# Filing stage of a graph layer: statistics of x two tiles ahead, and the preparation of edge keys in four pieces

## The reference

```
xn = layernorm(x)                                  # (x - mean) / sqrt(var + 1e-5), per row
x  = x + gnn(xn, edges) + mix(xn)                  # two graph convolutions; linear attention, 8 heads
x  = x + ffn(layernorm(x))                         # 8 experts, top 2
# a graph convolution, over the edges in both directions:
agg = segment_sum(x[src], dst) / max(deg, 1)
y   = x @ W0 + b0 + agg @ W1 + b1
```

## Time and profile before

| | us |
|---|---|
| median of 3 runs | 2323.24 |
| lowest, highest | 2322.51, 2326.59 |
| the profiled execution | 2325.6 |
| its span | 2324.1 |
| filing stage in it, first `onehots` to last `ranks` | 38.28 to 392.74 |
| first matmul of the next stage (L2222) | 430.86 |

### The profile page before, as it was taken

How to read it: one execution, slowest core, us unless ns; L and a number is a source line. 1 busy time by engine, 2 the same in 40 slices (tenths; PEclk the granted TensorE clock), 3 DMA queues, 4 the chain that set the end, 5 groups by cost and what they waited for, 6 DMA issues and landing times.

```text
span 2324.1 us, 52608 instructions
## 1 busy us (share of the span) xinstructions
PE 2083.6 (90%) x15454; PEld 1319.6 (57%) x15455; DVE 1578.9 (68%) x4935; ACT 1196.7 (51%) x2466; POOL 372.9 (16%) x440
## 2 busy tenths in 40 slices
PE   2766778999999999999689999999999996899996
PEld 1655566565555555555344544444444443799996
DVE  6888877799999999999555453545544555355554
ACT  2555555355555555555365562444444443566664
POOL 2000000000000000000011110121122112366665
PEclk9898899899999999999899999999999998899998
DMA  2222223622222222222343335555555554665552
GB/s 78 78 67 70 74 74 102 193 117 117 112 114 118 112 116 115 111 112 115 118 152 127 124 120 202 207 193 188 204 198 190 195 206 138 175 97 93 89 92 46
DMA packets 158449, 299.19 MB, mean 129 GB/s; under 512 B 31614, under 2 KB 107695, under 8 KB 156131
## 3 DMA queue, kind: packets, MB, share of 16 engines
q1 hardware_dynamic: 130787, 243.71, 30.4%
q0 software_dynamic: 25856, 47.15, 9.2%
q10 hardware_dynamic: 1664, 6.35, 0.8%
HBM read 148.37 MB, written 144.19 MB: 126 GB/s over the span
## 4 chain that ended last, share of the span: by engine, by line
PE 74%; issue 9%; DVE 6%; ACT 2%; POOLq 2%; DVEq 2%; DMA 2%; POOL 1%; ACTq 1%; SPq 0%
PE bank L2231 45%; PE bank L2222 6%; PE bank L2447 6%; PE bank L2432 6%; POOLq L832 2%; PE bank L2100 2%; PE bank L2414 1%; PE bank L2064 1%; PE bank L2074 1%; PE bank L2239 1%; PE bank L2379 1%; DVEq L1099 1%; ACT big L1782 1%; DMA big<-rows_dram 1%; PE bank L2085 1%
## 5 line engine op out<-in xcount | busy, mean ns | idle before, releaser
L2231 PE MATMUL bank<-RW,big 128*128 128x512 f16 x4802 | 1159.6, 380 | 4.9 <-DMA big<-a_dram 4.7
L2231 PEld LDWEIGHTS bank<-RW,big 128*128 128x128 f16 x4802 | 436.3, 98 | 395.8 <-issue 9.1
L1880 ACT ACTIVATE big<-bank 128x512 f16<-128x512 f32 (+1 forms) x640 | 364.1, 573 | 316.1 <-PE bank L2222 314.7
L1258 DVE TENSOR_TENSOR big<-iotaB,keys 128x512 f16<-128x512 f16 x1300 | 451.7, 416 | 7.9 <-issue 6.6
L2222 PEld LDWEIGHTS bank<-big 128*128 128x128 f16 x2560 | 191.0, 98 | 105.8 <-issue 1.4
L2222 PE MATMUL bank<-big 128*128 128x128 f16 x2560 | 247.5, 219 | 0.1
L964 POOL DMA_INDIRECT out_dram<-big x112 | 180.8, 1614 | 111.7 <-ACT big L2025 77.1
L900 POOL DMA_DIRECT2D big<-in_L_ffn_W_dram x8 | 6.4, 802 | 1117.2 <-DVE R L1317 1115.6
L2016 ACT ACTIVATE big<-bank,b1A,iscA 128x256 f32<-128x256 f32 x224 | 114.3, 560 | 100.4 <-PE bank L2432 95.1
L2447 PE MATMUL bank<-RW,big 128*128 (+1 forms) x1344 | 157.7, 274 | 0.0
L2432 PE MATMUL bank<-big,RW 128*128 128x256 f16 x1344 | 157.0, 274 | 0.4 <-ACT big L2005 0.4
(11 more groups left out here) (420 smaller groups left out, 2942.9 us busy)
## 6 DMA issues: line engine op xcount, KB each, us to landing
big<-a_dram SPq DMA_DIRECT2D x49, 800.0 KB, 6.0
big<-a_dram SPq DMA_DIRECT2D x49, 768.0 KB, 4.5
a_dram<-big SPq DMA_DIRECT2D x49, 640.0 KB, 3.0
a_dram<-big SPq DMA_DIRECT2D x49, 512.0 KB, 2.6
a_dram<-big SPq DMA_DIRECT2D x49, 416.0 KB, 2.4
big<-rows_dram SPq DMA_DIRECT2D x56, 265.0 KB
big<-in_x_dram SPq DMA_DIRECT2D x96, 128.0 KB, 2.1
own_dram<-big SPq DMA_DIRECT2D x48, 256.0 KB, 2.5
```

The lines of the kernel that those rows point to most:

```text
L1258: last = v.tensor_tensor(out[q].rearrange("p b (m k) -> p b m k", k=2), inturn(iotaB[:, :], QB, P // 2), twice(kd[:, q * QB:(q + 1) * QB, ...
L1880: a.activation(Ab[q][:, 0:n], banks[BB(q)][:, 0:n], ACT.Copy).then_inc(s_ab, 1)
L2231: last = mm(bank[:, :], blk(q, c), R2[:, u * 2 * D:(u + 1) * 2 * D], start=(i == 0), stop=(i == T - 1))
```

## The change

The statistics of x are computed two tiles ahead. `sums`, `rstd` and `offs` get two copies, x gets three buffers, and SP loads tile t + 3 after `normal1(t)`. ACT's order becomes `normal1(t)`, high part, `base1(t+1)`, `table1(t-1)`, `own1(t-3)`, `deviation1(t+2)`, `place1(t)`, low part. DVE takes `inverse(t+1)` after `ranks(t)` instead of `inverse(t)` ahead of `onehots(t+1)`.

`prepare` is cut in four: `words1`, `keys1`, `same1`, `within1`. In each group they follow the third, fourth, fifth and sixth tile, one each. Keys go to `keyw`, where each tile's 20 keys have 20 entries of -1 ahead of them, so that one comparison whose first operand reads overlapping ranges (`before`: for a shift d and an edge c, entry d + c) finds only earlier edges. The mask `earlier` and the multiplication with it are gone, on POOL its two instructions too; the sum over 20 shifts is two additions of halves and a reduction over 5 entries, which lie 20 apart.

```diff
-        xin = [sp1.f32(D) for _ in range(2)]
+        xin = [sp1.f32(D) for _ in range(3)]
...
@@ SP, tile t
-                if t + 2 < T:
+                if t + 3 < T:
                     sp.wait_ge(s_xn, t + 1)
...
-                        sp.dma_start(xin[t % 2], io["x"][(t + 2) * P:(t + 3) * P, :]).then_inc(s_x[t % 2], 16)
+                        sp.dma_start(xin[t % 3], io["x"][(t + 3) * P:(t + 4) * P, :]).then_inc(s_x[t % 3], 16)
...
@@ DVE
-                v.tensor_tensor(key1[:, sl], tF, movF, ALU.add)
+                v.tensor_tensor(keyw[:, :, CAP:2 * CAP], tile(tF), tile(movF), ALU.add)
...
-                for i in range(PACK):
-                    ks = slice(g * NK + i * CAP, g * NK + (i + 1) * CAP)
-                    v.tensor_tensor(same[:, i * CAP * CAP:(i + 1) * CAP * CAP].rearrange("p (a m k) -> p a m k", a=CAP, k=2),
-                                    inturn(key1[:, ks], CAP, CAP // 2), twice(key2[:, ks, :], CAP, CAP // 2), ALU.is_equal)
-                dve.drain()
-                v.tensor_tensor(ahead.rearrange("p (i n) -> p i n", i=PACK),
-                                same.rearrange("p (i n) -> p i n", i=PACK),
-                                wide(earlier[:, :], [P, PACK, CAP * CAP]), ALU.mult)
...
-                v.tensor_tensor(sv, av[:, :, 0:CAP // 2], av[:, :, CAP // 2:CAP], ALU.add)
...
-                v.tensor_tensor(sv[:, :, 0:4], sv[:, :, 0:4], sv[:, :, 6:10], ALU.add)
...
-                v.tensor_reduce(within[:, sl], sv[:, :, 0:6], AX.X, ALU.add)
...
+            def same1(g):
...
+                before = bass.AP(first.tensor, first.offset, [[pitch, P], [2 * CAP, PACK], [1, AHEAD], [1, CAP]])
+                v.tensor_tensor(same, before,
+                                keyw[:, :, CAP:2 * CAP].rearrange("p t (a c) -> p t a c", a=1)
+                                .to_broadcast([P, PACK, AHEAD, CAP]), ALU.is_equal)
...
+            def within1(g):
...
+                n = AHEAD
+                while n > 5:
+                    h = n - n // 2
+                    v.tensor_tensor(same[:, :, 0:n - h, :], same[:, :, 0:n - h, :], same[:, :, h:n, :], ALU.add)
+                    dve.drain()
+                    n = h
+                v.tensor_reduce(tile(within[:, g * NK:(g + 1) * NK]),
+                                same[:, :, 0:n, :].rearrange("p t d c -> p t c d"), AX.X, ALU.add)
...
             def inverse(t):
                 dve.wait_ge(s_std, t + 1)
-                if t:
-                    dve.wait_ge(s_xn, t)
+                if t >= 2:
+                    dve.wait_ge(s_xn, t - 1)
...
             for t in range(T):
-                inverse(t)
+                g, i = t // PACK + 1, t % PACK
                 if t + 1 < T:
                     onehots(t + 1, (t + 1) % 2)
                 ranks(t, t % 2)
-                if t % PACK == PACK // 2 and t // PACK + 1 < NG:
-                    prepare(t // PACK + 1)
+                if t + 1 < T:
+                    inverse(t + 1)
+                if g < NG:
+                    if i == 2:
+                        words1(g)
+                    if i == 3:
+                        keys1(g)
+                    if i == 4:
+                        same1(g)
+                    if i == 5:
+                        within1(g)
...
@@ ACT
-            base1(0)
-            deviation1(0)
+            deviation1(0)
+            deviation1(1)
+            base1(0)
             for t in range(T):
+                normal1(t)
                 if t + 1 < T:
                     base1(t + 1)
                 if t:
                     table1(t - 1)
-                parts1(t)
+                if t >= 3:
+                    own1(t - 3)
+                if t + 2 < T:
+                    deviation1(t + 2)
+                place1(t)
+                low1(t)
```

More of the change, by code:

```diff
@@ L34 @@
 CAP = 20
+AHEAD = CAP - CAP % 2
 WIN = P * CAP
@@ L120, in gps_layer @@
         uF, tF, badF, ownF, movF = (wr.f32(NK) for _ in range(5))
-        key1 = wr.f16(T * CAP)
+        keyw = wr.f16(PACK * 2 * CAP).rearrange("p (t c) -> p t c", c=2 * CAP)
         key2, ends = (wr.f16(T * CAP * 2).rearrange("p (c k) -> p c k", k=2) for _ in range(2))
@@ L125, in gps_layer @@
         at_pairs = wr.at
-        same = wr.f16(PACK * CAP * CAP)
-        ahead = wr.f16(PACK * CAP * CAP)
+        same = wr.f16(PACK * AHEAD * CAP).rearrange("p (t d c) -> p t d c", t=PACK, c=CAP)
         wr.at = at_pairs
@@ L414, in gps_layer @@
         s_edges = sem("s_edges")
-        s_x = [sem("s_x0"), sem("s_x1")]
+        s_x = [sem(f"s_xin{i}") for i in range(3)]
         s_xz = sem("s_xz")
@@ L564, in _ @@
                          io["dst"][(P - 1) * E:EDGES].rearrange("(a n) -> a n", a=1)).then_inc(s_edges, 16)
-            sp.dma_start(xin[0], io["x"][0:P, :]).then_inc(s_x[0], 16)
-            sp.dma_start(xin[1], io["x"][P:2 * P, :]).then_inc(s_x[1], 16)
+            for t in range(3):
+                sp.dma_start(xin[t], io["x"][t * P:(t + 1) * P, :]).then_inc(s_x[t], 16)
             def stretch(t):
@@ L775, in _ @@
             nc.gpsimd.memset(ones16, 1.0)
-            nc.gpsimd.memset(earlier[:, :], 1.0)
             nc.gpsimd.memset(flip[:, :], 0.0)
@@ L1043, in _, with tile, words1 @@
             v.tensor_scalar(winI[:, :], winF[:, :], 0.0, float(EDGES - WIN), ALU.max, ALU.min).then_inc(s_start, 1)
-            def prepare(g):
+            def tile(ap):
+                return ap.rearrange("p (t c) -> p t c", c=CAP)
+            def words1(g):
                 sl = slice(g * NK, (g + 1) * NK)
@@ L1058, in prepare, with keys1 @@
                 dve.drain()
-                def tile(ap):
-                    return ap.rearrange("p (t c) -> p t c", c=CAP)
+            def keys1(g):
+                sl = slice(g * NK, (g + 1) * NK)
                 mine = deep(tiles[:, g * PACK:(g + 1) * PACK], [P, PACK, CAP])
@@ L1085, in prepare @@
-                dve.drain()
-                v.tensor_tensor(sv[:, :, 0:4], sv[:, :, 0:4], sv[:, :, 6:10], ALU.add)
-                dve.drain()
-                v.tensor_reduce(within[:, sl], sv[:, :, 0:6], AX.X, ALU.add)
+            def same1(g):
+                first = keyw[:, :, CAP - AHEAD:2 * CAP]
+                pitch, _ = first.ap[0]
+                before = bass.AP(first.tensor, first.offset, [[pitch, P], [2 * CAP, PACK], [1, AHEAD], [1, CAP]])
+                v.tensor_tensor(same, before,
+                                keyw[:, :, CAP:2 * CAP].rearrange("p t (a c) -> p t a c", a=1)
+                                .to_broadcast([P, PACK, AHEAD, CAP]), ALU.is_equal)
+                dve.drain()
@@ L1184, in _ @@
             v.memset(xs[:, D:D + 1], 1.0)
-            prepare(0)
+            v.memset(keyw, -1.0)
+            inverse(0)
+            words1(0)
+            keys1(0)
+            same1(0)
+            within1(0)
             onehots(0, 0)
             for t in range(T):
-                inverse(t)
+                g, i = t // PACK + 1, t % PACK
                 if t + 1 < T:
@@ L1781, in normal1, with low1 @@
                 act.wait_ge(s_xt, t + 1)
-                a.activation(xs[:, 0:D], xin[t % 2], ACT.Identity, scale=rstd[:, :], bias=offs[:, :]).then_inc(s_xn, 1)
+                i = t % 2
+                a.activation(xs[:, 0:D], xin[t % 3], ACT.Identity, scale=rstd[:, i:i + 1], bias=offs[:, i:i + 1])\
+                 .then_inc(s_xn, 1)
                 act.drain()
-            def parts1(t):
-                normal1(t)
-                a.activation(R2[:, bass.ds(t * 2 * D, D)], xs[:, 0:D], ACT.Copy, scale=S).then_inc(s_xhi, 1)
-                if t >= 3:
-                    own1(t - 3)
-                if t + 1 < T:
-                    deviation1(t + 1)
-                place1(t)
-                a.activation(R2[:, bass.ds(t * 2 * D + D, D)], banks[5][:, D:2 * D], ACT.Copy, scale=S).then_inc(s_xlo, 1)
-            base1(0)
-            deviation1(0)
-            for t in range(T):
+                a.activation(R2[:, bass.ds(t * 2 * D, D)], xs[:, 0:D], ACT.Copy, scale=S).then_inc(s_xhi, 1)
+            def low1(t):
+                a.activation(R2[:, bass.ds(t * 2 * D + D, D)], banks[5][:, D:2 * D], ACT.Copy, scale=S).then_inc(s_xlo, 1)
+            deviation1(0)
+            deviation1(1)
+            base1(0)
+            for t in range(T):
+                normal1(t)
                 if t + 1 < T:
```

38 lines of the change are left out of this document (17 added, 21 removed).

## The result

| | before | after |
|---|---|---|
| median, us | 2324.31 (4 runs) | 2269.36 (4 runs) |
| lowest, highest | 2322.51, 2326.59 | 2268.29, 2270.74 |
| span of the profiled execution | 2324.1 | 2266.6 |

The ratio is 0.9763, 95% interval 0.9747 to 0.9780: 55 us faster. The two spans differ by 57.5 us, and the three timelines place it so: the first one-hots begin 4.5 us sooner (38.28, now 33.74), the filing stage is 49.7 shorter, the 38.1 us from there to the next stage's first matmul are 37.6, and what follows is 1890.5 instead of 1893.2.

A forecast was written before the change was run, and what follows sets the result against it. The filing stage was taken as a serial loop over engines, DVE waiting for ACT's root and PE for the normalised tile. 37.2 + 13.1 + 2.2 + 2.5 - 1.5 - 1.5 = 52.0 us off 2323.2: 2271, rounded to 2272; range 2264 to 2295.

The forecast's parts named there:

- Who sets the pace: Filing stage, plain tile after the change: DVE's 5.02 us is longest, against PE's 4.64 and ACT's 4.23.
- The wait for the root, 37.2: Filing stage: DVE's 37.2 us in front of the reciprocal, for ACT's square root, go with statistics computed a turn ahead.
- The rival in which it only changes its name: DVE waits at `ranks` for counts as long as for the root before; about 2306 to 2318 us, 5 in 100.
- The preparation, 7.75: One preparation on DVE costs 7.75 us, 2.18 less than before; six in the loop save 13.1 us.
- rival of dear forms: Preparation on DVE: overlapping comparison one element at a time, spaced reduction slow, or both; 2278 to 2289 us, 18 in 100.
- The moved waits: Loads around the stage: `words1(1)` waits for tile 13's window, 1.5 us once (0 to 4); `inverse(0)` costs nothing or under 1.
- The start, 2.2: First preparation, ahead of the loop on the only path: 2.2 us less; POOL's two dropped instructions hidden in the load wait.
- The end, 2.5: Between DVE's last ranks and the decoding: PE is now ahead, so 2.5 us off, between 0 and 4.
- The clock, 1.5: PE's clock falls after pauses in the filing stage: 1.5 us leaks through over the whole stage.
- rival of a late PE: Spread pauses drop PE's clock repeatedly and its 4.8 us of allowed lateness don't cover it; 22 us, so 2293, 11 in 100.
- slower case: Pauses hold PE at the lower clock for most of the filing stage; up to 2420 us, 3 in 100.
- signs named ahead: Filing stage: no DVE root wait, DVE busy over 93%, 49 to 52 us shorter, tile 5.0, comparison 1.6, reduction 0.9 us.

The follow-up runs named there:

- the pair of blocks: All four preparation pieces put in one block after the fourth tile: on the old statistics order with new preparation, 2308.28 us; on the new kernel, 2267.56 us.

## Why the prediction was right, step by step

**Who sets the pace: right.** 5.02 for DVE against 4.64 and 4.23 said that DVE would. The work added to DVE shows in full, the work added to the others doesn't, and DVE waits for them 0.6 us in the whole stage. The tile came to 4.94, not 5.02. From the start of the last instruction of `ranks` to the start of the reciprocal it is 0.91 us now (121.82 to 122.73) and was 0.98 in the tile of the earlier trace rows (58.61 to 59.59). That is nearly all of the 0.08 a tile, 4 us in all, in no term of the sum; the trace names no cause.

**The wait for the root, 37.2: right**, and nothing was late in its place. The rival in which it only changes its name fell: DVE's wait for counts is 0.3 us. That the cutting hides nothing was right too, for the new order alone. The reason given, that the low clock's 2.7 us a group are in the 37.2 already, is borne out by the pair of blocks: with the old order the cut gives 9 us, with the new none.

**The preparation, 7.75: too low by the reduction.** Its instructions by shape (busy us, mean ns of one):

```profile
L1077 DVE TENSOR_TENSOR R<-R 128x2800 f16<-128x2800 f16 x7 | 11.8, 1684 | 0.1
L1090 DVE TENSOR_REDUCE R<-R 128x140 f32<-128x700 f16 x7 | 9.7, 1389 | 0.5
L1087 DVE TENSOR_TENSOR R<-R 128x1400 f16<-128x1400 f16 x7 | 6.2, 882 | 0.1
L1087 DVE TENSOR_TENSOR R<-R 128x700 f16<-128x700 f16 x7 | 3.7, 525 | 0.5
```

The comparison took 1.68 against 1.69 taken and 3.07 feared: half of its shifted ranges begin at an odd element, and it ran like the mask of the earlier trace rows. This agrees with the Trainium skill (Vector Engine (DVE) Microarchitecture Reference, "5.1 Performance modes"), which found no effect of alignment for two sources, and not with the Trainium skill's VectorE: DVE Perf Modes, "Mode 2×_1P". The reduction took 1.39 against 0.88: 0.51 more, within the bound of 0.9 but not the value taken. It is near the estimate of 0.5 that the prediction worked out from the Trainium skill (Vector Engine (DVE) Microarchitecture Reference, "5.2 Measured stream behaviour"), whose figures are for 4-byte words and two sources. So the reduction's half of the rival of dear forms was true, 7 x 0.51 = 3.6 us. In DVE's timeline the pieces of one group take 1.53 (94.61 to 96.14), 1.92, 1.75 and 3.03 (114.99 to 118.02), 8.23 in all, 0.48 over the prediction's 7.75: the reduction is the whole of the miss.

**The moved waits.** The wait for window 13 was 0.25 us, not 1.5: the load's descriptor was issued by 48.83, and the words began at 50.28. `inverse(0)` was said to be hidden by the words' load. It stands right ahead of the words now:

```profile
24.76 0.16 DVE L1147 RECIPROCAL rstd<-sums 128x1 f32<-128x1 f32 x1 [8.06 <-ACT sums L1796]
25.00 0.16 DVE L1149 TENSOR_TENSOR offs<-sums,rstd 128x1 f32<-128x1 f32 x1
25.07 0.23 DVE L1047 TENSOR_SCALAR R<-R 128x140 int32<-128x140 int32 x1
```

DVE came for ACT's root, and 0.31 us lie between. In the two kernels with the old order, whose `inverse(0)` comes later, DVE waits there for the load until 24.74 and 24.82, so it had landed about then, and some 0.3 us are lost: under the 1 us that the prediction allowed.

**The start, 2.2: one step wrong.** "POOL's two dropped instructions are hidden in the same wait" failed. The load that the first words wait for was itself behind them (ACT issues its first window load at 17.34, before at 20.21): the words begin 3.07 us sooner (28.14, now 25.07), and the run that puts the two instructions back returns 2.9 of it. The first preparation itself gave 1.5 (10.14, now 8.67), less than 2.2, by the reduction again.

**The end, 2.5: wrong**, 0.5. DVE's wait behind its last ranks:

```profile
343.08 0.25 DVE L1135 TENSOR_SCALAR big<-big 80x364 int16<-80x364 int16 x1 [4.58 <-ACT big L1765]
```

It is 4.58 where the earlier trace rows have 5.24. PE wasn't ahead at the end: two tiles earlier (329.33) ACT's evacuation at L1781 had waited 2.6 us for an earlier store to finish, and PE 2.1 us for ACT. The trace before has the same two waits (2.5 and 2.0 us, at 386.60), which the prediction didn't read. Nor is the order of the statistics what sets this end: in the other kernels' traces DVE's wait there is 1.3 to 7.1 us, and 2.5 in both with the old order and the new preparation.

**The clock, 1.5: nothing leaked that can be seen.** The falls are there, 13 in the stage, and PE's room covers them; the kernel with more ScalarE work has 4 and the same stage, and the one with a single block stands longer at the lower level, with a stage that is no longer. The rival of a late PE is out: DVE never waits for it beyond 0.3 us at the counts, and TensorE took some 10 us more without lengthening the stage. So is the slower case: the mean granted clock is 0.92 over the stage.

**How 52 became 55.** The terms that fall in the stage give 37.2 + 13.1 - 1.5 - 1.5 = 47.3 us, a stage of 307.2 (the 304 of the prediction's check leaves the two 1.5 out); it took 304.8, 2.4 less. For it are the tile's 4 us and the smaller waits (1.25 and 1.5), against it the dearer preparation in the loop (6 x 0.48 = 2.9); 1.3 us are left over without a name. The start gave 4.5 where 2.2 were counted, the end 0.5 for 2.5. Behind the stage 2.7 us went, which is within what that part varies by. Together that is 57.5, the difference of the two spans; the medians differ by 55. The mechanism was right, but that the sum came within 3 us is in part luck: the misses of the terms, up to 4 us each, had both signs.

**Of the signs named ahead,** two did not come. DVE is busy 0.90 of the stage, not over 0.93: with 0.6 us of waits for other engines it is the engine that the stage follows, but busy time leaves out the short gaps between its instructions, which the figure of 0.93 had forgotten. And the reduction was not at 0.9.

## What to carry to other kernels

Work out the serial need of each engine per turn and take away waits first for the engine that needs most: here 37 us went by computing one tile further ahead, with two copies of a few columns and one more buffer. Cutting the block into pieces was worth 9 us while another engine's lateness still came back as a wait, and nothing once the cut-up engine set the pace. Two remedies for one wait didn't add up, so price the second with the first in place. When an engine sets the pace, look for anything small on it that an idle engine can do later and slower: 0.31 us a tile gave some 14 us in all.

## What the runs showed of the hardware

**Start-up.** Two GpSimd instructions of 0.43 and 0.66 us, whose result nothing at the start reads, moved the first preparation by some 2.9 us. With them other instructions changed length. Timelines, before:

```profile
7.19 1.90 DVE L1019 TENSOR_SCALAR shift<-back,third 128x49 f32<-128x49 f32 x1
9.16 2.81 DVE L1022 TENSOR_TENSOR R<-tiles,R 128x2548 f16<-128x2548 f32 x1
```
```profile
9.39 2.74 POOL L810 TENSOR_SCALAR_AFFINE_SELECT big<-big 128x64 f32<-128x64 f32 x1
```

After, the same instructions:

```profile
6.20 0.41 DVE L1014 TENSOR_SCALAR shift<-back,third 128x49 f32<-128x49 f32 x1
6.68 2.81 DVE L1017 TENSOR_TENSOR R<-tiles,R 128x2548 f16<-128x2548 f32 x1
```
```profile
8.44 1.21 POOL L805 TENSOR_SCALAR_AFFINE_SELECT big<-big 128x64 f32<-128x64 f32 x1
```

With the two put back, both long forms return:

```profile
7.18 1.90 DVE L1019 TENSOR_SCALAR shift<-back,third 128x49 f32<-128x49 f32 x1
```
```profile
9.38 2.74 POOL L810 TENSOR_SCALAR_AFFINE_SELECT big<-big 128x64 f32<-128x64 f32 x1
```

The part by which `shift` starts later, 1 us, has its wait: DVE waits for GpSimd's `flip`, and that stood behind `earlier`. Of the other 1.9 us (1.49 in `shift` and 0.38 in a later cast that took 0.72 and takes 0.34) the trace names no cause. GpSimd's select ends 0.16 us after DVE's comparison of 2548 elements in both kernels (12.13 and 11.97; 9.65 and 9.49), as if it couldn't run beside it. Both traces also have the reverse: a DVE cast of two elements (L1030, now L1025) takes 2.01 us and ends just behind GpSimd's memset of 2548 elements (17.83 and 17.81 before; 14.97 and 14.94 after). The Trainium skill (GPSIMD Engine Reference, "1. Specifications") says that the two engines share their interfaces to SBUF and contend when a DVE instruction has two inputs there or runs in a two-port mode; the pairs of ends fit that, and no run here tests it. Whether `shift` is four times as long by the same cause stays open.

**A reduction over spaced elements.** 700 two-byte elements, 20 apart, cost 1.39 us on VectorE, where 840 adjacent ones cost 1.03. Three additions that never leave unit step replaced it and took 0.41 us off each call (the piece is 2.62 us in place of 3.03).

**The clock.** In the kernel before it fell to the lower level beside pauses of 7 to 9.5 us, and once behind one of 2.75; in the new one it fell beside pauses of 1.5 to 5 us, but not beside each: TensorE waits 31 times for the one-hots and the clock falls 13 times, in the kernel with more ScalarE work 28 times and 4. The 13 are twelve of 3.41 us and one of 6.83; before there were 9, five of them 10.24 long and one 13.65, the last still under way at the stage's end. With the pieces the falls are more, and together shorter: 48 us of the stage against 75.
